# First layer of a four-layer graph network: W1 applied before the aggregate, row statistics tile by tile, attention masks made beside W2

## Chip, cores and metric

One core of a Trainium2 chip. The time is that of one execution on the device, in microseconds. The names of five engines recur: TensorE (PE; its weight loads are PEld), VectorE (DVE), ScalarE (ACT), GpSimd (POOL) and SyncE (SP), which here issues every DMA.

## The reference, cut to what matters

1250 nodes with 512 features, 40000 edges. Four layers follow each other; each takes h = relu(layernorm(x)) and adds its result to x. Only the first and the masks of the second matter here:

```python
h = jnp.maximum(_layernorm(x, axis=-1), 0.0)
agg = jax.ops.segment_sum(h[dst], src, num_segments=n)   # layer 0
y = (1.0 + eps) * h + agg
y = jax.nn.relu(y @ W1.T + b1)
y = y @ W2.T + b2
x = x + layernorm(y) * gamma + beta
# layer 1: softmax over the edges of a node, with q, k, v from relu(layernorm(x))
e = jnp.einsum('ehd,ehd->eh', k[src], q[dst]) / np.sqrt(DK)
```

The sum over edges is linear: with C the 1250x1250 matrix of edge counts, y = ((1 + eps) I + C) h, and so y W1 = ((1 + eps) I + C) (h W1).

## The kernel before, in words

The nodes lie in T = 10 tiles of 128 rows (the last has 98). Everything is f32 but the one-hot rows of the build. Each engine has its own program, executed in its order; they meet at semaphores. All DMAs go through SyncE's one queue in the order of its program.

**Setup (0 to 57 us).** SyncE loads the edges, constants, all of x and W1 (L287 to L309). VectorE (L869 to L985) works out from the edge list which edges each of 80 windows of the count matrix needs: casts, compares, ranges, 32 one-hot rows (L912), three products with parts of the edge weights over 125x10240 (L942). Small matmuls (L421 to L446) help it. ScalarE makes Exp of the weights and copies the keys (L1241, L1244), then for all tiles the row sums of x (L1250), behind VectorE's mean for all tiles (L947) all squares (L1254), one root (L1257), and, behind VectorE's reciprocal (L966), all ten Relu rows into H (L1261).

**Build (57 to 284 us).** For 40 groups of four half-windows TensorE multiplies one-hot rows (L459), VectorE makes the rows just ahead (L1000, L1008), ScalarE copies windows out of PSUM into buffers in X (L1285), SyncE moves each to DRAM (`edge_parts`, L317) and reads the counts back into CD (L326, L328).

**Aggregate (284 to 370 us).** TensorE multiplies H by the counts with 1 + eps on the diagonal (L493), for each of the four feature blocks f in three banks of PSUM; ScalarE copies each into `at` (L1292). Beside it GpSimd adds, tile by tile, the three parts of the edge weight sums (L1454, L1456); SyncE loads them (L332) and writes them back (`edge_sums`, L353). The stage buffers alternate, three in X and three in R0.

**W1 (371 to 405 us).** `feature_major` (L497, L504) multiplies `at` by W1, ScalarE evicts with Relu and bias into HT (L1306). In the gaps ScalarE computes Ln of the counts (L1300, into one of four buffers `lnc_raw`) and VectorE turns them into the additive masks of layer 1 (L1040, L1041), in place in CD. VectorE first puts the diagonal back (L1036).

**W2 with its tail (406 to 485 us).** `node_tiles` (L510 on) loops over the tiles: W2 matmuls of tile t (L531) into four banks in turn, the transposes of h of tile t-6 (L569), the V projection of tile t-7 (`values`, L587). VectorE's loop (from L1065) does per iteration t: add b2 out of PSUM (L1070) and statistics of tile t, the scale of t-1, gamma of t-2 (L1061), statistics of x of t-3, its scale of t-4. ScalarE's `tail` (L1327 on): root of t (L1267), Identity with scale of t-1 (L1314), root of x of t-3, Relu of x of t-4 (L1274), copy of the transposes of t-6 (L1322), copy of V of t-7 (L1349). GpSimd adds beta and updates x (L1462, L1465). x had been overwritten by window buffers and stage buffers, and is loaded again (`x_back`).

At 485.5 us the Q and K projections of layer 1 begin (L597); layers 1 to 3 aren't touched by the change.

Of the kernel before, what the change touches and what calls it, by code (L numbers as in the profile page):

```python
# [74 lines left out]
def rows(t):  # L75
    return min(P, N - t * P)
# [21 lines left out]
def build(nc, A, out):  # L98
# [4 lines left out]
    with ExitStack() as ctx:  # L103
# [52 lines left out]
        def bank(b, n=BANK):  # L156
# [14 lines left out]
        stage = [[X[:, :, :].rearrange("p t o -> p (t o)")[:, q * NQ:(q + 1) * NQ] for q in range(3)],  # L171
                 [R0[:, o:o + NQ] for o in (2048, 8840, 10092)]]
# [89 lines left out]

        def m_at(t):

            return (4 * BANK + t * 256) if t < 4 else (t - 4) * 256
# [17 lines left out]
        def _(sp):  # L283
            def rep(name, n):
                return A[name].rearrange("(a n) -> a n", a=1).to_broadcast([P, n])

            sp.dma_start(srcI, A["src_cols"]).then_inc(sem("edges_in"), 16)  # L287
            sp.dma_start(dstI, A["dst_cols"]).then_inc(sem("edges_in"), 16)
            sp.dma_start(ew, A["weight_cols"]).then_inc(sem("edges_in"), 16)
            sp.dma_start(growI, A["dst_rows"]).then_inc(sem("edges_in"), 16)  # L290
            sp.dma_start(K1[:, :], A["k1"][:, 0:NK1]).then_inc(sem("edges_in"), 16)
            sp.dma_start(K2, A["k2"]).then_inc(sem("edges_in"), 16)
            sp.dma_start(iota, A["iota"]).then_inc(sem("edges_in"), 16)
            sp.dma_start(key_base, A["k1"][:, NK1:NK1 + 2 * NW]).then_inc(sem("edges_in"), 16)
            def load_x(name):
                sp.dma_start(X[:, 0:T - 1, :], A["x"][0:(T - 1) * P, :].rearrange("(t p) f -> p t f", p=P))\
                    .then_inc(sem(name), 16)
                sp.dma_start(X[0:rows(T - 1), T - 1, :], A["x"][(T - 1) * P:N, :]).then_inc(sem(name), 16)

            load_x("x_in")  # L300
            sp.dma_start(bias_col[:, 0:4], A["L0_b1"]).then_inc(sem("x_in"), 16)
            sp.dma_start(bias_col[:, 4:6], A["L1_b1"]).then_inc(sem("x_in"), 16)
            sp.dma_start(bias_col[:, 6:7], A["L0_eps"].to_broadcast([P, 1])).then_inc(sem("x_in"), 16)
            for k in range(2):
                sp.dma_start(bias_col[:, 7 + k:8 + k], A["L2_bm"][k * P:(k + 1) * P].rearrange("(p o) -> p o", o=1))\
                    .then_inc(sem("x_in"), 16)


            sp.dma_start(wa4, A["L0_W1T"].rearrange("(k p) o -> p k o", p=P)).then_inc(sem("l0_w1_in"), 16)  # L309
# [31 lines left out]
            sp.wait_ge(sem("l0_h"), T)  # L341
            load_parts(0)


            sp.wait_ge(sem("base_used"), BASES * NG)
            sp.dma_start(wb4, A["L0_W2T"].rearrange("(k p) o -> p k o", p=P)).then_inc(sem("l0_w2_in"), 16)
            for i, n in enumerate(("L0_b2", "L0_gamma", "L0_beta")):
                sp.dma_start(bc0[:, i, :], rep(n, D)).then_inc(sem("l0_bc_in"), 16)

            load_parts(1)  # L350
            for t in range(T):
                sp.wait_ge(sem("tile_summed"), t + 1)
                sp.dma_start(dram_w[t * P:(t + 1) * P, :], stage[t % 2][0][:, 0:N]).then_inc(sem("w_out"), 16)  # L353
                if t + 2 < T:
                    sp.wait_ge(sem("w_out"), 16 * (t + 1))
                    load_parts(t + 2)
                elif t == T - 2:
                    sp.wait_ge(sem("w_out"), 16 * (t + 1))
                    sp.wait_ge(sem("eps_out"), T)
                    load_x("x_back")  # L360


            sp.wait_ge(sem("l0_h1_ps"), KF)
# [9 lines left out]
            load_qk(1)  # L373
            sp.wait_ge(sem("l0_mm"), T)
# [9 lines left out]
            for i, n in enumerate(("L1_ln1_g", "L1_ln1_b", "L1_ln2_g", "L1_ln2_b", "L1_b2")):  # L384
                sp.dma_start(bc1[:, i, :], rep(n, D)).then_inc(sem("l1_bc_in"), 16)
# [1153 lines left out]
```

## Time and profile before

| | us |
|---|---|
| median of 3 runs (1258.36 to 1259.93) | 1258.97 |
| profiled execution | 1256.01 |
| its span, first to last instruction | 1254.1 |
| TensorE busy | 1102.4 (88%) |
| VectorE busy | 646.8 (52%) |
| ScalarE busy | 419.7 (33%) |
| GpSimd busy | 144.0 (11%) |
| mean granted clock of TensorE | 0.954 of 2.4 GHz |

A busy share over the whole span says little, since the stages have different limits; the rows further down are read stage by stage. The chain of waits follows, from the last instruction back, what released each step. Idle time of an engine off that chain costs nothing.

### The profile page before, as it was taken

The page shows a single profiled execution, that of the slowest core. Times are in us where ns is not written, and L with a number is a line of the kernel's source. Part 1 is how long each engine was busy: PE and PEld are TensorE (multiplying, and loading weights), DVE is VectorE, ACT ScalarE, POOL GpSimd, SP SyncE. Part 2 cuts the span into 40 slices and gives each one's busy share as a digit, 9 for nine tenths or more (in the row PEclk, how much of TensorE's full clock was granted, in tenths as well). Part 3 has the DMA queues.
Part 4 walks back from the last instruction along what each step waited for, and adds up shares of the span by engine and source line. Part 5 has one row for each costly group of instructions (what it writes and reads, how often), then busy time and mean ns, then how long its engine had stood idle before and what let it go on. Part 6 is the DMA issues. An engine that isn't in the chain of part 4 may idle for free.

```text
span 1254.1 us, 17427 instructions
## 1 busy us (share of the span) xinstructions
PE 1102.4 (88%) x5880; PEld 698.9 (56%) x5880; DVE 646.8 (52%) x1835; ACT 419.7 (33%) x711; POOL 144.0 (11%) x112
## 2 busy tenths in 40 slices
PE   1378877779999999989999999999996998899998
PEld 0134444445555445547777777776453798555543
DVE  6877787784017840026666666665619525700033
ACT  2501233330006341016555555555234523610000
POOL 0000000002654440000000000001315403000000
PEclk9998777779999999999999999999999998999999
DMA  5001467778886111100000000005301005000001
GB/s 153 0 0 42 129 173 208 201 213 269 274 281 210 56 34 34 34 0 1 2 1 2 1 1 2 2 1 178 119 1 34 9 13 194 34 1 1 9 33 40
DMA packets 67233, 93.65 MB, mean 75 GB/s; under 512 B 5145, under 2 KB 56032, under 8 KB 67158
## 3 DMA queue, kind: packets, MB, share of 16 engines
q1 hardware_dynamic: 67158, 92.65, 23.4%
q8 instruction: 48, 0.79, 0.3%
q14 instruction: 27, 0.22, 0.1%
HBM read 58.03 MB, written 34.60 MB: 74 GB/s over the span
## 4 chain that ended last, share of the span: by engine, by line
PE 72%; DVE 12%; DMA 6%; issue 5%; ACT 3%; SPq 2%; DVEq 0%; ACTq 0%
PE PS L459 8%; PE PS L669 7%; PE PS L493 7%; PE PS L652 7%; PE PS L817 7%; PE PS L626 7%; PE PS L852 5%; DMA edge_parts<-X 5%; PE PS L597 5%; PE PS L531 5%; PE PS L504 3%; PE PS L587 3%; DVE R L1117 2%; PE PS L779 2%; PE PS L799 2%
## 5 line engine op out<-in xcount | busy, mean ns | idle before, releaser
L459 PE MATMUL PS<-HT,R 125*128 125x313 bf16 (+1 forms) x636 | 178.5, 419 | 61.2 <-DVE HT L1000 27.5
L459 PEld LDWEIGHTS PS<-HT,R 125*128 x636 | 103.5, 171 | 137.0 <-issue 103.9
L1106 DVE CUSTOM_DVE_ANT_0 HT<-PS,CD 128x1250 f32<-128x1250 f32 (+1 forms) x80 | 116.3, 1454 | 55.2 <-issue 55.2
L652 PE MATMUL PS<-K,HT 128*128 128x128 f32 (+2 forms) x800 | 112.5, 280 | 15.0 <-DVE R L1117 14.4
L1008 DVE TENSOR_SCALAR HT<-BC,HT 125x314 f16 x316 | 102.0, 364 | 35.9 <-PE PS L459 30.9
L1382 ACT ACTIVATE HT<-HT,soft 128x1250 f32<-128x1250 f32 (+1 forms) x80 | 107.1, 1338 | 19.7 <-DVE soft L1109 12.6
L1285 ACT COPY X<-PS 128x626 f32<-128x626 f32 x80 | 53.6, 689 | 167.9 <-PE PS L459 102.9
L652 PEld LDWEIGHTS PS<-K,HT 128*128 128x128 f32 (+2 forms) x800 | 84.0, 140 | 43.1 <-DVE R L1117 23.6
L1362 ACT COPY R<-PS 128x512 f32<-128x512 f32 (+1 forms) x120 | 64.8, 574 | 121.5 <-PE PS L652 119.5
L626 PE MATMUL PS<-R 64*128 64x512 f32 (+3 forms) x480 | 95.8, 531 | 4.8 <-DVE soft L1106 3.1
L669 PE MATMUL PS<-R 128*64 128x128 f32 (+2 forms) x1600 | 94.3, 273 | 0.0
L493 PE MATMUL PS<-CD,H 128*128 128x512 f32 (+2 forms) x240 | 86.0, 521 | 3.7 <-issue 3.7
L669 PEld LDWEIGHTS PS<-R 128*64 128x64 f32 (+1 forms) x1600 | 84.8, 137 | 6.4 <-issue 5.8
L1117 DVE COPY R<-PS 128x512 f32<-128x512 f32 (+1 forms) x80 | 54.3, 678 | 65.2 <-PE PS L652 65.2
L817 PE MATMUL PS<-R,H 128*128 128x512 f32 (+2 forms) x240 | 85.2, 513 | 0.0
L1000 DVE TENSOR_SCALAR HT<-BC 125x314 bf16<-125x314 f16 x320 | 72.8, 299 | 13.9 <-PE PS L459 9.7
L626 PEld LDWEIGHTS PS<-R 64*128 64x128 f32 (+1 forms) x480 | 61.2, 185 | 32.0 <-issue 23.3
L1228 DVE SCALAR_TENSOR_TENSOR R<-PS,invdeg,BC 128x512 f32<-128x512 f32 (+1 forms) x10 | 7.5, 749 | 132.9 <-PE PS L852 132.9
L493 PEld LDWEIGHTS PS<-CD,H 128*128 128x128 f32 (+1 forms) x240 | 46.1, 192 | 43.4 <-issue 43.2
L597 PE MATMUL PS<-HT,R 128*128 128x512 f32 (+1 forms) x192 | 67.3, 513 | 0.0
L817 PEld LDWEIGHTS PS<-R,H 128*128 128x128 f32 (+1 forms) x240 | 45.0, 190 | 38.7 <-issue 38.4
L597 PEld LDWEIGHTS PS<-HT,R 128*128 128x128 f32 x192 | 36.5, 190 | 31.2 <-issue 31.1
(211 smaller groups left out, 1357.1 us busy)
## 6 DMA issues: line engine op xcount, KB each, us to landing
edge_parts<-X SPq DMA_DIRECT2D x160, 156.5 KB, 3.5
X<-edge_parts SPq DMA_DIRECT2D x15, 626.0 KB, 5.6
R<-edge_parts SPq DMA_DIRECT2D x15, 626.0 KB, 5.7
CD<-edge_sums SPq DMA_DIRECT2D x1, 6250.0 KB, 20.9
CD<-edge_parts SPq DMA_DIRECT2D x10, 469.5 KB, 4.5
CD<-edge_parts SPq DMA_DIRECT2D x3, 1565.0 KB, 11.6
X<-in_x SPq DMA_DIRECT2D x2, 2304.0 KB
edge_sums<-X SPq DMA_DIRECT2D x5, 625.0 KB, 6.2
```

Of the source, the lines that this page charges most:

```text
L459: return mm(bank(b0 + h, QUART), stat, hot, start=first, stop=True, skip_group_check=True)
L493: i = mm(bank(b0 + j, sn), H[0:rows(t), t, f * P:(f + 1) * P], cd[0:rows(t), t, s0:s0 + sn], start=t == 0, stop=t == T - 1, skip_group_che ...
L597: i = mm(bank(3 * m + j, sn), wqk[p % 2][:, m, k, :], ht[:, k, s0:s0 + sn], start=k == 0, stop=k == KF - 1)
L626: i = mm(PS[0:n, a * N + s0:a * N + s0 + sn], qT[a * DK:(a + 1) * DK, p, t * P:t * P + n], kT[a * DK:(a + 1) * DK, p, s0:s0 + sn], start=T ...
L652: m = nc.tensor.transpose(PS[0:rows(j), o:o + n], Pb[u % 2][a][0:n, j * P:j * P + rows(j)], ident[0:n, 0:n])
L669: m = mm(PS[a * DK:(a + 1) * DK, o:o + n], V[0:rows(j), j, (2 * p + a) * DK:(2 * p + a + 1) * DK], PT[c % RING][0:rows(j), (2 * jj + a) * ...
L817: i = mm(bank(3 * (f % 2) + j, sn), H[0:rows(t), t, f * P:(f + 1) * P], cs[0:rows(t), t, s0:s0 + sn], start=t == 0, stop=t == T - 1)
L1000: ve.tensor_scalar(src_oh[:, base_slot(w, q * GH + h), :], iota[0:EC, :], base_key[:, q, v:v + 1], None, ALU.is_equal).then_inc(sem("base_ ...
L1008: i = ve.tensor_scalar(late_oh[:, bass.ds(m & (GEN - 1), 1), h, :].rearrange("p a n -> p (a n)"), iota[0:EC, :], key_base[0:EC, v:v + 1], ...
L1106: ve.tensor_tensor_reduce(Pb[s][a][0:n], PS[0:n, a * N:(a + 1) * N], cd[0:n, t, :], 1.0, -3e38, ALU.add, ALU.max, soft[0:n, s, a:a + 1]).t ...
L1117: ve.tensor_copy(PT[c % RING].rearrange("p (j n) -> p j n", j=4)[:, :, 0:n], bank(6 + c % 2).rearrange("p (j n) -> p j n", j=4)[:, :, 0:n])\
L1382: sc.activation(Pb[s][a][0:n], Pb[s][a][0:n], ACT.Exp, bias=soft[0:n, s, 2 + a:3 + a], accum_out=zsum[0:n, z + a:z + a + 1]).then_inc(sem( ...
```

## The change

- The setup's loads are reordered: edges and x in parts (tiles 0 and 1, then W1, then tiles 2 to 4, then the rest); iota and key bases come last.
- Row statistics tile by tile: ScalarE sum, square and root, GpSimd the mean and its product with the reciprocal, VectorE the reciprocal (`unit_scale`), ten calls spread through its setup. The products L942 are cut in halves, a `unit_scale` between each pair.
- W1 moves: each tile of h is transposed (`turn_h`), copied to `h_t` and multiplied by W1, ten tiles, with the setup's small matmuls between them; ScalarE copies the result over H. `feature_major` is gone. The aggregate's eviction is the Relu with bias, straight into HT.
- ScalarE's Exp and key copies come after the fifth iteration of its loop over tiles.
- The build begins with banks 4 to 7; its second group waits for all ten tiles of h W1.
- The Ln calls stand in `tail` of W2 (`beside=lnc`), one per tile, and VectorE's mask of tile t at the end of its iteration t.
- The stage buffers of the sums lie in R0 alone, so tiles 0 to 6 of x are loaded again right behind the last counts; the weights of V, Q and K are loaded before the loop of the sums.

The diff, cut to its core:

```diff
+            def turn_h(t):
+                n = rows(t)
+                pe.wait_ge(sem("l0_h"), t + 1)
+                if t > 0:
+                    pe.wait_ge(sem("h_t"), t)
+                for k in range(KF):
+                    i = nc.tensor.transpose(bank(3)[:, k * P:k * P + n], H[0:n, t, k * P:(k + 1) * P], ident[0:n, 0:n])
+                i.then_inc(sem("h_t_ps"), 1)
+
+            pe.wait_ge(sem("l0_w_in"), 16)
+            turn_h(0)
+            for t in range(T):
+                n = rows(t)
+                if t + 1 < T:
+                    turn_h(t + 1)
+                pe.wait_ge(sem("h_t"), t + 1)
+                if t >= 2:
+                    pe.wait_ge(sem("hw"), t - 1)
+                for k in range(KF):
+                    i = mm(bank(t % 2)[0:n], h_t[t % 2][:, k, 0:n], wa4[:, k, :], start=k == 0, stop=k == KF - 1)
+                i.then_inc(sem("hw_ps"), 1)
+                if t == 1:
+                    ranges()
+                if t == 2:
+                    trips_per_group()
+                if t == 3:
+                    trip_ends()
+                if t == 5:
+                    gathered_keys()
...
+                if w == 1:
+                    pe.wait_ge(sem("hw"), T)
...
+            def unit_scale(t):
+
+                n = rows(t)
+                dve.wait_ge(sem("x_std"), t + 1)
+                ve.reciprocal(x_std[0:n, t:t + 1], x_std[0:n, t:t + 1]).then_inc(sem("x_rstd"), 1)
...
+                for h in range(2):
+                    j = 2 * SUB * h
+                    i = ve.tensor_tensor(dst_oh[0:EC, (q + 1) * 4 * SUB + j:(q + 1) * 4 * SUB + j + 2 * SUB, :],
+                                         dst_oh[0:EC, j:j + 2 * SUB, :], wpart[q].unsqueeze(1).to_broadcast(shape), ALU.mult)
+                    if h == 0:
+                        unit_scale(7 + q)
...
+            def mask(t):
+
                 n = rows(t)
                 dve.wait_ge(sem("lnc_raw"), t + 1)
...
+                if t < T:
+                    mask(t)
+            dve.wait_ge(sem("lnc"), T)
...
+            for t in range(T + 5):
+                if t < T:
+                    n = rows(t)
+                    act.wait_ge(sem(x_part(t)[0]), x_part(t)[1])
+                    sc.activation(H[0:n, t, :], X[0:n, t, :], ACT.Copy, accum_out=x_sum[0:n, t:t + 1]).then_inc(sem("x_sum"), 1)
+                if 1 <= t <= T:
+                    u = t - 1
+                    n = rows(u)
+                    act.wait_ge(sem("x_nmean"), u + 1)
+                    sc.activation(H[0:n, u, :], X[0:n, u, :], ACT.Square, bias=x_nmean[0:n, u:u + 1],
+                                  accum_out=x_sq[0:n, u:u + 1]).then_inc(sem("x_sq"), 1)
+                    act.wait_ge(sem("x_sq"), u + 1)
+                    sc.activation(x_std[0:n, u:u + 1], x_sq[0:n, u:u + 1], ACT.Sqrt, scale=1.0 / D, bias=gate[0:n, 1:2])\
+                        .then_inc(sem("x_std"), 1)
+                if 2 <= t < T + 2:
+                    u = t - 2
+                    n = rows(u)
+                    act.wait_ge(sem("x_norm"), u + 1)
+                    sc.activation(H[0:n, u, :], X[0:n, u, :], ACT.Relu, bias=x_nmr[0:n, u:u + 1], scale=x_std[0:n, u:u + 1])\
+                        .then_inc(sem("l0_h"), 1)
+                if 3 <= t < T + 3:
+                    u = t - 3
+                    n = rows(u)
+                    act.wait_ge(sem("h_t_ps"), u + 1)
+                    if u >= 2:
+                        act.wait_ge(sem("hw_ps"), u - 1)
+                    sc.copy(h_t[u % 2][:, :, 0:n], bank(3).rearrange("p (k n) -> p k n", k=KF)[:, :, 0:n])\
+                        .then_inc(sem("h_t"), 1)
+                if 4 <= t < T + 4:
+                    u = t - 4
+                    n = rows(u)
+                    act.wait_ge(sem("hw_ps"), u + 1)
+                    sc.copy(H[0:n, u, :], bank(u % 2)[0:n]).then_inc(sem("hw"), 1)
+                if t == 4:
+                    weights()
...
-                sc.copy(at[:, f, 0:N], PS[:, 3 * (f % 2) * BANK:3 * (f % 2) * BANK + N]).then_inc(sem("l0_agg_ev"), 1)
+                sc.activation(ht[:, f, 0:N], PS[:, 3 * (f % 2) * BANK:3 * (f % 2) * BANK + N], ACT.Relu,
+                              bias=bias_col[:, f:f + 1]).then_inc(sem("l0_h1_ev"), 1)
...
-            tail("l0", "l1_xn", "l1_h", lag=LAG0, after=v_out)
+            tail("l0", "l1_xn", "l1_h", beside=lnc, lag=LAG0, after=v_out)
...
+            def center(t):
+                n = rows(t)
+                pool.wait_ge(sem("x_rstd"), t + 1)
+                gp.tensor_tensor(x_nmr[0:n, t:t + 1], x_nmean[0:n, t:t + 1], x_std[0:n, t:t + 1], ALU.mult)\
+                    .then_inc(sem("x_norm"), 1)
+
+
+
+            for t in range(T):
+                n = rows(t)
+                pool.wait_ge(sem("x_sum"), t + 1)
+                gp.tensor_scalar(x_nmean[0:n, t:t + 1], x_sum[0:n, t:t + 1], -1.0 / D, None, ALU.mult)\
+                    .then_inc(sem("x_nmean"), 1)
+                if t >= 1:
+                    center(t - 1)
+            center(T - 1)
```

## Rows read from the trace of the kernel before

**Rows 1.** Stretches: span, busy PE, PEld, DVE, ACT, POOL, clock, DMA share, GB/s

```profile
290.00:300.00 10.00, 10.00 (x29) 5.23 (x28) 5.78 (x35) 0.00 (x0) 0.41 (x1) 1.00 1.02 354
...
406.40:485.50 79.10, 75.42 (x201) 34.72 (x202) 43.70 (x125) 32.06 (x61) 25.74 (x20) 0.98 0.12 40
...
438.00:441.00 3.00, 3.00 (x5) 1.19 (x4) 1.90 (x7) 1.99 (x5) 2.20 (x2) 0.53 0.02 5
```

**Rows 2.** Chain that ended last, in order of time: start, us, what

```profile
369.81 1.21 ACT R L1292
371.15 33.83 PE PS L504 x96
...
406.45 13.98 PE PS L531 x32
...
446.31 0.44 PE PS L569 x4
446.75 3.44 PE PS L587 x8
...
485.50 67.16 PE PS L597 x192
```

**Rows 3.** Timeline of the setup: start, us, engine, line, operation [idle before]

```profile
16.48 0.49 DVE L890 SCALAR_TENSOR_TENSOR HT<-HT 125x320 f32<-125x320 f32 x1
...
20.50 0.63 ACT L1250 ACTIVATE H<-X 128x512 f32<-128x512 f32 x1
...
41.98 0.72 ACT L1254 ACTIVATE H<-X,invdeg 128x512 f32<-128x512 f32 x1 [15.25 <-DVE invdeg L947]
...
57.21 1.29 PE L459 MATMUL PS<-HT,R 125*128 125x313 bf16 x4 [16.83 <-DVE HT L1000]
```

**Rows 4.** Groups by shape, 406 to 485.5 us: busy us, mean ns

```profile
L531 PE MATMUL PS<-R,HT 128*128 128x512 f32 x72 | 31.5, 593 | 1.5 <-ACT HT L1306 1.5
...
L1349 ACT COPY R<-PS 128x512 f32<-128x512 f32 x9 | 5.3, 586 | 13.1 <-PE PS L587 13.1
```

**Rows 5.** Group by shape, 0 to 57 us: busy us, mean ns

```profile
L446 PE MATMUL PS<-CD 128*125 128x320 f32 x4 | 2.5, 780 | 1.5 <-DVE CD L936 1.5
```

**Rows 6.** TensorE's timeline in the build and in the W2 stage

```profile
103.48 4.26 PE L459 MATMUL PS<-HT,R 125*128 x16 [0.38 <-issue]
...
437.51 5.37 PE L587 MATMUL PS<-WA,HT 128*128 128x512 f32 x8 [2.48 <-ACT HT L1322]
```

**Rows 7.** Who waited for whom, 160 to 284 us: total, times, longest

```profile
ACT X L1285 <- DMA edge_parts<-X: 64.8, 44, 4.0
```

**Rows 8.** ScalarE's timeline around the two table loads

```profile
381.22 1.28 ACT L1300 ACT_TABLE_LOAD   x1
382.52 3.80 ACT L1300 ACTIVATE R<-CD,gate 128x1250 f32<-128x1250 f32 x3
...
407.55 1.28 ACT L1267 ACT_TABLE_LOAD   x1
```

**Rows 9.** GpSimd's timeline: the last tile's sums

```profile
387.37 3.75 POOL L1454 TENSOR_TENSOR R<-R 128x1252 f32<-128x1252 f32 x1 [4.98 <-DMA R<-edge_parts]
391.20 3.30 POOL L1456 TENSOR_TENSOR R<-R 128x1252 f32<-128x1252 f32 x1
```

**Rows 10.** Timeline of the W2 stage: an add and its Identity

```profile
413.59 0.69 DVE L1070 TENSOR_TENSOR R<-PS,BC 128x512 f32<-128x512 f32 x1 [0.40 <-PE PS L531]
...
415.72 0.81 ACT L1314 ACTIVATE R<-R,rs 128x512 f32<-128x512 f32 x1
```

**Rows 11.** VectorE's timeline: the masks

```profile
383.89 0.81 DVE L1040 TENSOR_SCALAR CD<-CD 128x1250 f32<-128x1250 f32 x1 [9.81 <-ACT R L1300]
384.73 1.46 DVE L1041 TENSOR_TENSOR CD<-CD,R 128x1250 f32<-128x1250 f32 x1
...
388.33 3.47 DVE L1040 TENSOR_SCALAR CD<-CD 128x1250 f32<-128x1250 f32 x1
391.83 3.99 DVE L1041 TENSOR_TENSOR CD<-CD,R 128x1250 f32<-128x1250 f32 x1
```

More of the change, by code:

```diff
@@ new lines, in gathered_keys @@
+            def gathered_keys():
+                pe.wait_ge(sem("setup_dve"), 9)
+                for k in range(3):
+                    i = mm(bank(4)[0:EC, 0:FIX * 2 * NW], key_t[0:KC[k], k, :], pick[0:KC[k], k, :, :], start=k == 0, stop=k == 2)
+                i.then_inc(sem("setup_ps"), 1)
+            def turn_h(t):
[6 more added lines that the diff above has]
+                i.then_inc(sem("h_t_ps"), 1)
@@ L929, in _ @@
             link(ve.tensor_copy(wpart[2], rem2))
+            unit_scale(6)
             dve.wait_ge(sem("setup_ps"), 6)
@@ L1237, in _ @@
             sc = nc.scalar
-            act.wait_ge(sem("setup_dve"), 5)
-            sc.activation(we, ew, ACT.Exp, bias=wmx[:, 3:4]).then_inc(sem("we"), 1)
-            act.wait_ge(sem("setup_ps"), 4)
-            for k in range(3):
-                i = sc.copy(key_t[0:KC[k], k, :], bank(3)[0:KC[k], k * P:k * P + EC])
-            i.then_inc(sem("key_t"), 1)
-            act.wait_ge(sem("x_stats_free"), 1)
-            act.wait_ge(sem("x_in"), 7 * 16)
-            for t in range(T):
-                n = rows(t)
-                sc.activation(H[0:n, t, :], X[0:n, t, :], ACT.Copy, accum_out=x_sum[0:n, t:t + 1]).then_inc(sem("x_sum"), 1)
@@ L1251, in _, with weights @@
-            act.wait_ge(sem("x_nmean"), 1)
-            for t in range(T):
-                n = rows(t)
-                sc.activation(H[0:n, t, :], X[0:n, t, :], ACT.Square, bias=x_nmean[0:n, t:t + 1],
-                              accum_out=x_sq[0:n, t:t + 1]).then_inc(sem("x_sq"), 1)
-            act.wait_ge(sem("x_var"), 1)
-            sc.activation(x_std[:, :], x_sq[:, :], ACT.Sqrt).then_inc(sem("x_std"), 1)
-            act.wait_ge(sem("x_norm"), 1)
-            for t in range(T):
-                n = rows(t)
-                sc.activation(H[0:n, t, :], X[0:n, t, :], ACT.Relu, bias=x_nmr[0:n, t:t + 1], scale=x_std[0:n, t:t + 1])\
-                    .then_inc(sem("l0_h"), 1)
+            def weights():
+                act.wait_ge(sem("setup_dve"), 5)
+                sc.activation(we, ew, ACT.Exp, bias=wmx[:, 3:4]).then_inc(sem("we"), 1)
+                act.wait_ge(sem("setup_ps"), 4)
+                for k in range(3):
+                    i = sc.copy(key_t[0:KC[k], k, :], bank(5)[0:KC[k], k * P:k * P + EC])
+                i.then_inc(sem("key_t"), 1)
```

185 lines of the change are left out of this document (83 added, 102 removed).

## The prediction

> **What bounds the kernel now.** I read the table by stage first [rows 1]: in every stage from 57 us to the end TensorE is the busiest engine, but the chain of waits [rows 2] shows which stretches are really TensorE's. From 371.15 on it is, for 33.83 us: the matmuls of W1 (L504) run without a gap, then comes an eviction, and the W2 stage starts at 406.45. That stage ends when the projection starts, at 485.50, so it lasts 79.05 us; it is TensorE's by volume (75.4 us busy [rows 1]). Before 57 us the chain is VectorE's: the build's first matmul, at 57.21, had waited 16.83 us for it [rows 3]. So three stretches count: the setup (0 to 57.2), the W1 stage (371.3 to 406.45) and the W2 stage with its tail (79.05). The profiled execution took 1256.01 us (span 1254.1); the median of the timed runs is 1258.97, 2.96 more, and I add each change to both.
>
> **1. W1 leaves the path.** Today the aggregate's last eviction ends at 371.0, W1 starts at 371.15, W2 at 406.45 [rows 2]. After the change the aggregate's last eviction is already the Relu with bias (some 0.1 us longer) and W2 can start at 371.3. Gone: 35.2 us. The aggregate itself keeps its 240 instructions and its banks: 0.
>
> **2. The setup gets W1.** Ten tiles, each four transposes and four matmuls of 128x512 in two passes. Dense, a tile's eight matmul instructions take 3.44 us and four transposes 0.44 [rows 2]. At this place TensorE is slow, though: a two-pass matmul of 320 columns took 780 ns [rows 5], where 512 columns took 593 in the W2 stage [rows 4]; so the clock is at 1.2 GHz here, although the table prints 1.00 for it. The restart at 437.51 shows what dense work does then: eight instructions in 5.37 us [rows 6] at a granted clock of 0.53 [rows 1], the eight at 446.75 in 3.44 again [rows 2]. I take the first tile at 6.8, later ones at 3.44.
> TensorE executes in order, and all ten tiles stand ahead of the first group of the build, which starts at 57.21 today. ScalarE does per tile a sum (0.63), a square (0.72), a short root, the Relu (0.81, as the Identity of [rows 10]) and two copies out of PSUM (0.59 each) [rows 3, 4], about 3.6 us with the wait for its own accumulator; with three loads of the function table (1.28 each [rows 8]) for root, Exp and root, that is 40 us of its own. The first Relu waits for VectorE's first reciprocal (its place is ahead of the operation at 16.48 [rows 3]) and ends near 18; transposes, copy and a load of the third tile of x bring the first W1 matmul to 21.6. From there TensorE's queue holds 10 x 3.44 + 9 x 0.44 = 38.4 us, the small setup matmuls that are now between the tiles (eight for the ranges, four for the trips, two for the ends and six for the keys, some 6.4 by the 0.78 of [rows 5] for the six largest and their overlap), 2.4 of waits and 3.4 for the slow first tile: 72.2; of this the gathered keys give back about 1 at full clock. **The build starts near 71 instead of 57.2, +14**. VectorE doesn't cover this: its own chain ends 5 us later than now, because its fifth reciprocal waits for a root that ScalarE does behind the Exp and the key copies, and each of the ten reciprocals stands in front of work of the build's setup. The few small steps that VectorE loses and the two inputs fewer that it waits for save about 1, which is in the 5. Bounds: +9.5 (all tiles at full clock, no waits) to +22 (three tiles slow, waits twice as long). GpSimd's new 128x1 operations have no row; between nothing and 3.30 us, its row of 1252 columns [rows 9], and I take 0.2. The chain meets it twice, for the first and the last tile, so the start moves by 0 to 6; the upper bound holds that.
>
> **3. The build passes this on.** From 160 us on ScalarE waits for the window transfers, 64.8 us in 44 waits [rows 7], but a transfer can't begin before its window is built, so the late start isn't taken up there. The steps of the build are short groups of four matmuls with register work between; what a warmer TensorE gives them I count at 0 (at most 1 or 2 us, in the lower bound). The +14 arrives at the aggregate. Waiting for `hw` ahead of the second group costs nothing, since sixteen matmuls of the first group still run at 103.48 [rows 6].
>
> **4. The masks move into the W2 tail.** This is the largest term. Today Ln and masks lie beside W1: ScalarE loads the Ln table once at 381.22 and the root's at 407.55 [rows 8]. So Ln and root are in different tables, and a switch costs its load (381.22 to 382.50, Ln at 382.52). In the tail each tile has root, Identity, Ln, root: two loads per tile, twenty in all. Now the order of VectorE and ScalarE in one iteration, timed from VectorE's add on the PSUM bank (L1070): statistics, root and scale, then Identity from +2.13 to +2.94 (413.59, 415.72) [rows 10], load +1.28, Ln +1.27 (3.80 for three) [rows 8] gives +5.5; only then VectorE's mask, 0.81 and 1.46 [rows 11]; then the next add. With 0.1 of signalling **the iteration takes 7.85 us, where W2's matmuls need 3.44** [rows 2]. The second load and VectorE's remaining steps fit beside it. Of the two loads one is exposed.
> The sum: first add 3.7 after W2's start; ten iterations, the first without Identity, 77.5; then the values still to be done. TensorE's order is W2 tile t, transposes t-6, values t-7, and the values wait for a copy that ScalarE makes behind Ln; so values 3 to 9 lie behind the tenth iteration: 0.5 + 7 x 3.88 - 0.44 = 27.2. Together 108.4.
> To that comes GpSimd. The fourth iteration waits for its first update of x. Its sums end at 394.5 now; ahead of their loads now stand seven tiles of x (1.8 MB) and the V, Q and K weights (2 MB), while the queue already moves 354 GB/s [rows 1], some 11 us of transfer, of which I count 7.5 (the loop of sums waits on round trips and absorbs part), and 2 for GpSimd's operations that are stretched beside VectorE's, to 3.75 for one [rows 9]. At 404 it is free, the update is there at 406.7, the mask behind it 4.5 later than otherwise: +4.5 (0 to 10).
> VectorE and GpSimd hold each other up: the mask operations of 0.81 and 1.46 took 3.47 and 3.99 while the sums ran [rows 9, 11], +5.2 for one pair. Three pairs meet the sums, most of which ends in the wait just counted; later GpSimd's pair for the tile ends about when the mask begins. I take +3 (0 to 10).
> TensorE idles 22 us ahead of its eighth tile, 8 ahead of the first values and 4 ahead of the fourth; a restart costs 5.37 - 3.44 = 1.9 [rows 2, 6]. Two on the path, +3.8 (0 to 6), though one of today's is in the 79.05.
> **Tail: 108.4 + 4.5 + 3 + 3.8 = 119.7, against 79.05: +40.6** (+29 to +55).
>
> The Trainium skill, "SBUF — State Buffer" (SBUF: two separate sides), says that VectorE and GpSimd share one pair of ports and that an operation of the one that needs it holds it whole while the other blocks; by that the 3.47 and 3.99 are waits, not slower work, and the trace agrees: the first ends just behind the end of GpSimd's operation.
> The Trainium skill's "ScalarE: Activation LUTs" (What ACT_TABLE_LOAD costs; table sets) advises to do all calls of one set before switching, and prices a switch at about 2.66 us, 1.28 of load and 1.38 of drain. The rule speaks against this change; its load agrees with 1.28 here, its drain doesn't show between 381.22 and 382.52. By its price the tail would be an estimated 14 us longer.
>
> **Sum.** +14 - 35.2 + 40.6 = +19.4: 1275.4 for a profiled execution, **1278 us** for the median.
>
> **Rivals.**
> (a) *The masks fit into idle time.* For it: in the W2 stage VectorE is busy 43.7 of 79.1 us and ScalarE 32.1 [rows 1]; the moved work is 23 us on one and 13 + 23 on the other. If the engines ran ahead enough, the tail would grow by only some 6: 14 - 35.2 + 6 = -15, 1244 us. Against: each add stands behind the mask of the tile before in VectorE's order. 11 in 100.
> (b) *One of the costs is hidden:* the loads don't appear or lie in waits (ten exposed at 1.28: -12.8), or the setup's delay is taken up in the build (-14). 1265 us. 10 in 100.
> (c) *TensorE stays at 1.2 GHz through the setup.* Ten tiles at 6.9 + 0.8 put the start of the build at about 103: +46 instead of +14, 1310 us. It decides if the third tile still takes over 6 us. For it: sixteen matmuls in a row of 313 columns took 0.266 each at 103.48 [rows 6], which is 1.2 GHz, after 46 us of building without a pause of note. Against: those were short groups with gaps; dense matmuls woke up in one tile. 7 in 100.
> (d) *Both loads are exposed,* because the second root of the iteration is what the next add waits on: 10 x 1.28 more, 1291 us. 8 in 100.
> My forecast, 1262 to 1296 by its bounds, has 64 in 100.
>
> **Numbers.** Range 1260 to 1296: it leaves out (a) and (c), 18 in 100, and the sum of all upper bounds. About 0.2% (2.5 us) can be told from no change. Faster: (a) and a little of (b), 0.12. Same: the rest of (b) at its lower bounds, 0.04. Slower: 0.84.
>
> **What would show it.** The build's first matmul at 67 to 75 us; no L504, W2 starting 1.5 us behind the aggregate; twenty table loads in the tail and the adds at L1070 about 7.9 us apart for ten tiles; the projection starting some 115 to 122 us behind W2's start. Adds 4 to 5 us apart would mean (a), and my reading of the order was wrong; fewer loads (b); a third W1 tile over 6 us (c). If the aggregate starts less late than the build does, step 3 is wrong.

## The result: 27 us slower

The changed kernel takes 1285.32 us (median of four runs, 1284.29 to 1286.84) against 1258.66 us (1256.12 to 1259.93) for the kernel before on the same chip: ratio 1.0214, 95% interval 1.0193 to 1.0235. The forecast was 1278 us with a range of 1260 to 1296, so sign and range hold and the predicted time is 7.3 us too low. The profiled execution took 1285.58 us (span 1283.8) against 1256.01: +29.6, of which 2.7 is that the profiled run of before lay under its median.

**The profile after.** The table by stretch has the same columns as [rows 1]; the first stretch is what the setup grew by, the second a piece of it, the third the W2 stage with its tail.

```profile
57.21:76.72 19.51, 14.83 (x35) 6.62 (x34) 8.56 (x19) 4.63 (x8) 4.38 (x2) 0.83 0.00 0
...
64.00:69.00 5.00, 5.00 (x7) 1.98 (x7) 3.25 (x12) 0.58 (x1) 0.00 (x0) 0.57 0.00 0
...
390.70:515.04 124.34, 83.85 (x201) 37.70 (x202) 75.47 (x147) 67.69 (x89) 48.53 (x28) 0.82 0.25 82
```

In [rows 1] the W2 stage had TensorE busy for 75.4 of 79.1 us. Now it is busy for 84 of 124, VectorE for 75 and ScalarE for 68: no engine fills the stage, so it is an order of waits that sets it. The chain of waits shows which (start, us, what; it answers to [rows 2]).

```profile
398.00 1.28 ACT L1369
399.30 1.35 ACT R L1369
400.67 1.91 DVE CD L1084
402.60 3.98 DVE CD L1085
...
418.57 2.51 DVE rs L1022
...
439.38 1.28 ACT L1369
440.67 1.35 ACT R L1369
442.04 0.82 DVE CD L1084
442.88 1.46 DVE CD L1085
...
460.51 5.54 PE PS L620 x8
...
485.70 6.61 PE PS L620 x8
...
515.04 1.29 PE PS L630 x3
```

L1369 is the load of the Ln table and Ln itself, L1084 and L1085 are the masks, L1022 is a product of one column in VectorE's scale, L620 the V projection, L630 the projection that ends the stage. The chain that was TensorE's runs through ScalarE and VectorE for ten tiles. Where the 29.5 us up to the projection come from:

| stretch | before | after | difference | predicted |
|---|---|---|---|---|
| first matmul of the build | 57.21 | 76.72 | +19.5 | +14 |
| build, to the aggregate's start | 226.6 | 225.9 | -0.7 | 0 |
| aggregate and W1, to W2's start | 122.66 | 88.11 | -34.55 | -35.2 |
| W2 stage, to the projection | 79.05 | 124.34 | +45.3 | +40.6 |
| projection to the end of the span | 768.6 | 768.8 | +0.2 | 0 |

Two terms were too small, the setup by 5.5 us and the tail by 4.7. Both shortfalls have to do with GpSimd. For the setup, the timeline of the changed kernel (start, us, engine, line, operation, idle before):

```profile
50.26 2.80 DVE L992 TENSOR_TENSOR R<-R,BC 125x5120 bf16<-125x5120 bf16 x1
...
53.07 5.53 DVE L992 TENSOR_TENSOR R<-R,BC 125x5120 bf16<-125x5120 bf16 x2
53.22 8.36 POOL L1512 TENSOR_TENSOR valid<-invdeg,winv 128x1 f32<-128x1 f32 x2 [3.16 <-DVE winv L910]
...
58.60 2.79 DVE L992 TENSOR_TENSOR R<-R,BC 125x5120 bf16<-125x5120 bf16 x1
...
61.48 0.81 ACT L1314 ACTIVATE H<-X,valid,winv 128x512 f32<-128x512 f32 x1 [7.42 <-POOL valid L1512]
...
62.91 1.09 PE L473 MATMUL PS<-K,H 128*128 128x128 f32 x4 [4.68 <-ACT CD L1322]
...
63.79 5.86 PE L486 MATMUL PS<-WA,CD 128*128 128x512 f32 x8
...
69.83 7.06 PE L486 MATMUL PS<-WA,CD 128*128 128x512 f32 x16
...
76.72 1.53 PE L509 MATMUL PS<-HT,R 125*128 125x313 bf16 x10
```

GpSimd's product of one column (`center`, L1512) starts behind the ninth reciprocal and two of them take 8.36 us, until VectorE's last wide product has ended. The line's own view has the shortest, median and longest of its ten in ns:

```profile
L1512 POOL TENSOR_TENSOR valid<-invdeg,winv x10: 184/190/8224, 16.5 to 61.4; 128x1 f32<-128x1 f32 x9, 98x1 f32<-98x1 f32 x1
```

So the first of the two alone took 8.22 us and the second began at 61.4. ScalarE's Relu, which needs only the first, waits 7.42 us for it, TensorE waits 4.68, restarts near its lower level (granted clock 0.57 from 64 to 69 us, eight matmuls in 5.86 instead of 3.60 us), and still has two tiles ahead of the build.

### The profile page after: what moved, and what is told of

Same layout as the page of the kernel before. It is cut to its first block, busy times and chain, and to the rows that moved or that the text cites. A ratio compares the mean times of both kernels' runs of the same rounds, so it can differ in the third digit from the quotient of the medians.

```text
span 1283.8 us, 17580 instructions
## 1 busy us (share of the span) xinstructions
PE 1117.5 (87%) x5904; PEld 703.7 (55%) x5904; DVE 654.8 (51%) x1845; ACT 453.7 (35%) x756; POOL 160.4 (12%) x132
## 4 chain that ended last, share of the span: by engine, by line
PE 69%; DVE 12%; ACT 6%; DMA 6%; issue 5%; SPq 1%; POOL 1%; DVEq 0%; ACTq 0%
PE PS L509 8%; PE PS L702 7%; PE PS L542 7%; PE PS L685 7%; PE PS L850 7%; PE PS L659 6%; PE PS L885 5%; PE PS L630 5%; DMA edge_parts<-X 5%; PE PS L564 3%; PE PS L620 3%; DVE R L1163 2%; PE PS L812 2%; PE PS L832 2%; PE PS L486 2%
## 5 line engine op out<-in xcount | busy, mean ns | idle before, releaser
L509 PE MATMUL PS<-HT,R 125*128 125x313 bf16 (+1 forms) x636 | 176.1, 415 | 46.0 <-ACT X L1353 15.5
L1042 DVE TENSOR_SCALAR HT<-BC 125x314 bf16<-125x314 f16 x320 | 73.0, 299 | 16.0 <-PE PS L509 12.3
L630 PE MATMUL PS<-HT,R 128*128 128x512 f32 (+1 forms) x192 | 67.3, 513 | 0.0
L1529 POOL TENSOR_TENSOR R<-R 128x1252 f32<-128x1252 f32 x10 | 28.3, 2832 | 304.6 <-DMA R<-edge_parts 304.6
```

The lines of the kernel that those rows point to most:

```text
L509: return mm(bank(b0 + h, QUART), stat, hot, start=first, stop=True, skip_group_check=True)
L630: i = mm(bank(3 * m + j, sn), wqk[p % 2][:, m, k, :], ht[:, k, s0:s0 + sn], start=k == 0, stop=k == KF - 1)
L1042: ve.tensor_scalar(src_oh[:, base_slot(w, q * GH + h), :], iota[0:EC, :], base_key[:, q, v:v + 1], None, ALU.is_equal).then_inc(sem("base_ ...
```

## The experiments

All kernels below state the bound of the register on which the build waits by an assertion (`nc.s_assert_within(...)` instead of `.with_bounds(...)`). The first run, the changed kernel with nothing else, prices that and is what the others are compared with. The kernel before, timed beside them on each chip, took between 1258.4 and 1262.1 us (medians), so runs on different chips are compared by their ratios to it. "Stage" is the time from W2's first matmul to the projection's first in the timeline of the profiled execution; the timeline lets the projection start 0.16 us earlier than the chain, so the changed kernel's stage is 124.2 by this measure.

**control**

```diff
-                     v[VALUES * k + GH].with_bounds(min_val=w + k + 2, max_val=(w + k + 1) * (NC - FIX) + 1))
+                     nc.s_assert_within(v[VALUES * k + GH], min_val=w + k + 2, max_val=(w + k + 1) * (NC - FIX) + 1))
```

> The changed kernel itself, with one more assertion behind each load of a group's end in the build (40 groups, on TensorE and VectorE), which all kernels of these experiments carry. Every theory: within 0.2% of the changed kernel, 1283 to 1288 us, iterations of the W2 stage 7.83 us apart, the build's first matmul at 76.7. If it is faster or slower, the other experiments are read against it.

1288.8 us, ratio 1.0256 (1.0222 to 1.0289), 0.4% above the changed kernel's 1.0214 where at most 0.2% was expected. The build starts at 76.7 us as without the assertion, the aggregate 5.8 us later, and the stage is 121.3 us, 2.9 shorter: its first add comes 1.5 earlier and the intervals beside the sums are 0.9 shorter. So much a stage that collides with the sums varies from one kernel to the next.

**before_with_assertion**: the same edit in the kernel before.

> The kernel before with the bound of the register read in the build stated by an assertion, as in all these experiments, and nothing else: it prices what masks_in_tail_only carries. The control took 3.5 us over the changed kernel for it. If the assertion costs the build the same here, 1261 to 1264 us; in masks_in_tail_only the aggregate began 7.2 us later than in the kernel before, which would rather give 1264 to 1267 us.

1266.76 us beside 1262.05, ratio 1.0039 (1.0028 to 1.005). W2 starts at 415.3 and the stage is 78.9 us. So assertion against assertion the change costs 1.0256 / 1.0039 = 1.022, what it costs without (1.0214).

**masks_in_tail_only**: the kernel before with `mask(t)` at the end of the tail's loop on VectorE and `beside=lnc` in ScalarE's tail, W1 where it was.

```diff
-            for t in range(T):
+            def mask(t):
...
-            dve.wait_ge(sem("lnc"), T)
...
+                if t < T:
+                    mask(t)
...
-            tail("l0", "l1_xn", "l1_h", lag=LAG0, after=v_out)
+            tail("l0", "l1_xn", "l1_h", beside=lnc, lag=LAG0, after=v_out)
```

> The kernel before, with one part of the change alone: Ln in ScalarE's tail and the mask at the end of VectorE's iteration. Theory A (order: each add waits for the mask of the tile before, and that for root, Identity, table load and Ln): iterations 7.8 us apart for ten tiles, W2 stage 108 + 2 to 4 of restarts = 110 to 112 us instead of 79, so +31 to +33, 1290 us; here the sums of GpSimd end ahead of W2, so they can't be the cause. Rival B (the stage grew because GpSimd's sums and VectorE block each other): hardly any sum is left in the stage, it stays under 90 us, at most 1270 us. Rival C (the masks fit into idle time): 85 us, 1265 us.

1297.86 us, ratio 1.0317 (1.0284 to 1.035). W2 starts at 415.0, as in before_with_assertion, and the stage grows from 78.9 to 111.7 us. VectorE's timeline, masks and adds (L1070) of this kernel:

```profile
441.41 0.68 DVE L1070 TENSOR_TENSOR R<-PS,BC 128x512 f32<-128x512 f32 x1
...
447.02 0.81 DVE L1041 TENSOR_SCALAR CD<-CD 128x1250 f32<-128x1250 f32 x1 [1.92 <-ACT R L1303]
447.87 1.46 DVE L1042 TENSOR_TENSOR CD<-CD,R 128x1250 f32<-128x1250 f32 x1
449.24 0.69 DVE L1070 TENSOR_TENSOR R<-PS,BC 128x512 f32<-128x512 f32 x1
```

The adds are 7.83 us apart with W1 in its old place and the sums over 14 us before the stage begins; 111.7 is 3.3 more than the 108.4 that the prediction had for the bare order, ahead of its 3.8 for TensorE's restarts. The order of root, Identity, load, Ln and mask makes the pace, by itself. Masks in idle time (rival a, some 6 us) and both loads exposed (rival d, some 9.1 us an iteration) fall.

**ln_as_identity**

```diff
-                sc.activation(lnc_raw[t % 4][0:n], cd[0:n, t, :], ACT.Ln, bias=gate[0:n, 0:1]).then_inc(sem("lnc_raw"), 1)
+                sc.activation(lnc_raw[t % 4][0:n], cd[0:n, t, :], ACT.Identity, bias=gate[0:n, 0:1]).then_inc(sem("lnc_raw"), 1)
```

> The changed kernel with Identity in place of Ln (layer 1's masks leave the logarithm of the counts out; the operation's length is the same), so no function table changes in the W2 stage. Theory A with one exposed load per iteration: adds 6.55 us apart instead of 7.83, -12.8 us, 1272 us. Rival D (both loads of an iteration are exposed): 5.3 us apart, -25.6 us, 1260 us. Rival E (loads lie in waits): 7.8 apart, 1285 us.

1280.84 us, ratio 1.019 (1.0161 to 1.022), 8.0 us under the control; the expected 12.8 don't come. The adds stand 7.46 apart instead of 7.84, though a load of 1.28 is out of each iteration. Control first, then ln_as_identity (groups by shape on VectorE beside W2's tiles; busy us, mean ns):

```profile
L1084 DVE TENSOR_SCALAR CD<-CD 128x1250 f32<-128x1250 f32 x6 | 5.7, 952 | 11.1 <-ACT R L1369 11.1
```

```profile
L1084 DVE TENSOR_SCALAR CD<-CD 128x1250 f32<-128x1250 f32 x6 | 11.2, 1858 | 2.6 <-ACT R L1369 2.0
```

And the timeline of ln_as_identity, GpSimd's update of x and the mask:

```profile
434.96 1.26 POOL L1542 TENSOR_TENSOR X<-X,R 128x512 f32<-128x512 f32 x1
435.04 1.86 DVE L1084 TENSOR_SCALAR CD<-CD 128x1250 f32<-128x1250 f32 x1 [0.50 <-ACT R L1369]
```

The mask now begins 0.08 us after GpSimd's update of x began, and takes 1.86 us instead of 0.81: it ends 0.68 behind GpSimd's end. In the control the load held the mask back until GpSimd was done (its update ran from 436.56 to 437.82, the mask began at 438.07). The mask begins 1.43 us earlier in its iteration and takes 1.05 longer, so the iteration is 0.38 shorter. One load per iteration is on the path, as predicted, but it covered a collision. Most of what the run gained lies elsewhere. The stage is 8.5 us shorter, of which 1.4 lie in the eighth interval and 3.8 behind the tenth add. There TensorE waits 1.38 us ahead of the fourth value tile and 1.54 ahead of the fifth, instead of 3.70 ahead of the fourth, and the fourth takes 3.70 us instead of 6.43.

**sums_of_4_columns**: GpSimd's sums of the count parts run over 4 columns instead of 1252.

```diff
-                gp.tensor_tensor(s[0], s[0], s[1], ALU.add).then_inc(sem("sum_own"), 1)
+                gp.tensor_tensor(s[0][:, 0:4], s[0][:, 0:4], s[1][:, 0:4], ALU.add).then_inc(sem("sum_own"), 1)
```

> The changed kernel, with GpSimd's additions of the edge weight parts done on 4 of 1252 columns (the weights of layer 2 are left incomplete); loads and write-backs stay. Theory A plus port: the first three iterations shrink from 10.56, 10.15 and 11.95 us to 7, 7.9 and 7.9, the ten copies that restore the diagonal from 6.7 to 3 to 4 us: -9 to -13 us, 1274 us. Rival (those three are long for another reason, as the first update of x coming late behind its loads): under -4 us.

1282.61 us, ratio 1.0207 (1.0177 to 1.0237), 6.2 us under the control, between the two expectations; the stage is 113.7 us, 7.6 shorter. The 9 to 13 were worked out from the changed kernel, and the control loses 2.3 us less than it to collisions (its first add and the three intervals). The first three intervals are 6.97, 7.83 and 7.84 us, but the fourth is 9.41: there GpSimd's first two operations on x meet VectorE's one-column product (1.13 instead of 0.16 us) and its mask (1.42 instead of 0.81). Its first mask pair on VectorE, and behind it the same pair in the changed kernel:

```profile
402.22 0.81 DVE L1084 TENSOR_SCALAR CD<-CD 128x1250 f32<-128x1250 f32 x1 [2.92 <-ACT R L1369]
403.06 1.46 DVE L1085 TENSOR_TENSOR CD<-CD,R 128x1250 f32<-128x1250 f32 x1
```

```profile
400.67 1.90 DVE L1084 TENSOR_SCALAR CD<-CD 128x1250 f32<-128x1250 f32 x1 [2.92 <-ACT R L1369]
402.60 3.98 DVE L1085 TENSOR_TENSOR CD<-CD,R 128x1250 f32<-128x1250 f32 x1
```

**loads_earlier_alone**: SP's queue loads parts 1 and 2 of a sum as soon as their buffers are free, and x and the projection weights inside the loop of sums instead of ahead of it.

```diff
-            load_x(0, 7, "x_in0")
...
                 if t + 2 < T:
+                    load_parts(t + 2, (1, 2))
                     sp.wait_ge(sem("w_out"), 16 * (t + 1))
-                    load_parts(t + 2)
+                    load_parts(t + 2, (0,))
+                if t == 3:
+                    load_x(0, 7, "x_in0")
...
```

> The changed kernel with only the queue reordered as in and_loads_earlier; the masks stay in the W2 tail, nothing is left out. GpSimd's last sum should end some 12 us after W2's start (11.8 in all_three) instead of 31. Theory A (the masks set the tail's pace from the fourth tile on, the collisions with the sums only lengthen the first three iterations): iterations two and three lose the 2.3 to 3.7 us that each has over 7.84, the later ones stay 7.84 apart, the stage falls from 121.3 to 113 to 117 us and the run to 1280 to 1285 us, so the reordering is worth 16 us with the masks gone and only a third of that with them. Theory B (the tail waits for the sums' end even with the masks in it): the gain is the same 14 to 18 us, 1271 to 1275 us.

1285.45 us, ratio 1.0184 (1.0161 to 1.0207) against the control's 1.0256. The last sum ends 12.3 us behind W2's start (403.8) instead of 31.3, and the adds are 9.81, then 7.82 and 7.84 apart: the stage is 114.8 us, 6.5 shorter. In the profiled executions the projection starts at 518.6 us, in the control at 518.2, because the build is longer here, and the profiled execution (1290.18) is the slowest of its four (1282.75 to 1290.18); so the 0.7% that the run gains by its ratio can't be laid to the stage. GpSimd's timeline, its last sum and the first operation of the tail:

```profile
412.86 3.28 POOL L1534 TENSOR_TENSOR R<-R 128x1252 f32<-128x1252 f32 x1
428.06 1.26 POOL L1540 TENSOR_TENSOR R<-R,BC 128x512 f32<-128x512 f32 x1 [11.93 <-DVE R L1108]
```

GpSimd now waits 11.93 us for VectorE. With the masks in the tail, early sums are worth only the collisions that they avoid.

**masks_beside_projection**: Ln and masks move behind the tail, beside the Q and K projections, with two buffers for the logarithms.

```diff
-                if t < T:
-                    mask(t)
+            for t in range(2):
+                mask(t)
             for p in range(PAIRS):
                 dve.wait_ge(sem("k_ps"), p + 1)
                 ve.tensor_copy(kT[:, p, 0:N], PS[:, 3 * BANK:3 * BANK + N]).then_inc(sem("k_ev"), 1)
+                for t in ((2, 3, 4), (5, 6, 7), (8, 9), ())[p]:
+                    mask(t)
...
```

> The changed kernel with the masks taken out of the W2 tail and made beside the Q and K projections, where ScalarE and VectorE have only the evictions; nothing is left out of the computation. Theory A (the tail's pace is set by the masks): the adds after the third come some 4 to 6 us apart instead of 7.84, and the stage's end is then set by the sums of x, which end 33 us after W2's start and need nine more value tiles after them: about 97 us instead of 121.3 in the control, so the run falls by 24 us less what the masks give back beside the projections (0 to 8): 1265 to 1273 us. Theory B (the tail is set by the late loads of x and of the sums, not by the masks): the stage stays within 5 us of the control's and the run near 1285 us or above it.

1265.39 us, ratio 1.0037 (1.002 to 1.0053), 2.1% (27.5 us) under the control. The stage falls from 121.3 to 95.2 us. The first four adds are 3.36 to 3.44 apart, then one gap of 21.65 us comes, until x is updated, then three of 3.95 to 3.97. The sums' late end was hidden behind the masks and is the bound once they are gone. The table by stretch, the projections alone (columns as above):

```profile
495.50:562.40 66.90, 66.90 (x192) 36.28 (x191) 26.29 (x23) 19.32 (x16) 0.00 (x0) 1.00 0.10 32
```

TensorE is busy without a gap while VectorE works 26.3 and ScalarE 19.3 us beside it. The projections take 67.2 us with the masks beside them and without. From their start to the end of the span it is 770.2 us against the control's 769.1, so in this place the masks cost 1.1 us at most.

**and_loads_earlier**: masks_beside_projection with the queue of loads_earlier_alone.

> masks_beside_projection, and the queue reordered: the parts of the third and later sums are loaded as soon as their buffers are free, and x and the projection weights are loaded within the sums instead of ahead of them. If the sums' late end is what holds the tail once the masks are gone, the stage falls from about 97 to the 79 to 85 us that it had before the change, and the run by 10 to 18 us more: 1250 to 1262 us. If the sums are held by GpSimd's own time (two passes of about 3 us for each of ten tiles) and not by the loads, the run stays within 4 us of masks_beside_projection.

1249.7 us, ratio 0.9912 (0.9894 to 0.993); the stage is 79.6 us, about as long as before the change (78.9). The same reordering that took 6.5 us off the stage with the masks in it takes 15.6 us off without them.

**center_on_dve**: the product of one column follows VectorE's reciprocal on VectorE.

```diff
-                ve.reciprocal(x_std[0:n, t:t + 1], x_std[0:n, t:t + 1]).then_inc(sem("x_rstd"), 1)
+                link(ve.reciprocal(x_std[0:n, t:t + 1], x_std[0:n, t:t + 1]))
+                ve.tensor_tensor(x_nmr[0:n, t:t + 1], x_nmean[0:n, t:t + 1], x_std[0:n, t:t + 1], ALU.mult)\
+                    .then_inc(sem("x_norm"), 1)
```

> The changed kernel with the 128x1 product of the x statistics done by VectorE right behind its reciprocal instead of by GpSimd; nothing is left out. If GpSimd's small product, kept from the SBUF port by VectorE's products (8.36 us for two), is what makes the build start late, the first build matmul comes at 70 to 73 us instead of 76.7 and the run is 4 to 7 us under the control: 1282 to 1285 us. If the setup is late because of TensorE's lower clock or the later transfers, it stays within 1.5 us of the control's 1288.8 us.

1285.74 us, ratio 1.0203 (1.0186 to 1.022), 0.5% (6.7 us) under the control by the ratios. The timeline of the setup:

```profile
54.82 0.14 DVE L910 RECIPROCAL winv<-winv 128x1 f32<-128x1 f32 x1
55.00 0.16 DVE L911 TENSOR_TENSOR valid<-invdeg,winv 128x1 f32<-128x1 f32 x1
...
63.71 7.06 PE L486 MATMUL PS<-WA,CD 128*128 128x512 f32 x16
70.60 1.46 PE L509 MATMUL PS<-HT,R 125*128 125x313 bf16 x9
```

The product takes 0.16 us here and the build starts at 70.60, 6.1 us earlier. From 41 us on TensorE's tiles now follow each other almost without a gap.

**quarter_of_w1_product**: center_on_dve with one of the four feature blocks of the W1 product.

```diff
-                for k in range(KF):
-                    i = mm(bank(t % 2)[0:n], h_t[t % 2][:, k, 0:n], wa4[:, k, :], start=k == 0, stop=k == KF - 1)
+                i = mm(bank(t % 2)[0:n], h_t[t % 2][:, 0, 0:n], wa4[:, 0, :], start=True, stop=True)
```

> center_on_dve with three of the four feature blocks of the W1 product left out in the setup (2 matmuls for each tile instead of 8; the values are then wrong in that sense, the rest of the work is the same). Per tile TensorE loses 2.6 us, 26 us for the ten. If TensorE's stream sets the setup's end once the small product is off GpSimd, the build starts as soon as VectorE is ready, whose last setup operations end 64.3 us in center_on_dve and whose first build operation could start 2.5 to 3 us later: 67 to 68.5 us instead of 70.6, and the run is 2 to 3.5 us under center_on_dve's 1285.7. If TensorE sets nothing there, the start stays at 70.6 us; if TensorE also delays what VectorE waits for (its small products queue behind the tiles), the start falls below 66 us and the run below 1281 us.

1278.27 us, ratio 1.0129 (1.0106 to 1.0152), 0.7% (9.3 us) under center_on_dve. By its numbers it is the third outcome of the three: the build starts at 62.5 us, 8.1 earlier, so TensorE's tiles also delay what VectorE waits for. VectorE's and TensorE's timelines:

```profile
62.01 0.94 DVE L1043 TENSOR_SCALAR HT<-BC 125x314 bf16<-125x314 f16 x4 [2.53 <-issue]
...
62.47 1.01 PE L508 MATMUL PS<-HT,R 125*128 125x313 bf16 x4 [1.38 <-DVE HT L1043]
```

It is not TensorE's small products that VectorE waits for, as the expectation had it, but ScalarE's roots. Its reciprocals (`unit_scale`) in center_on_dve, ScalarE's copy of h W1 ahead of the second of these roots, and the first of the two reciprocals with a quarter of W1, where the second doesn't wait:

```profile
34.08 0.16 DVE L910 RECIPROCAL winv<-winv 128x1 f32<-128x1 f32 x1 [4.33 <-ACT winv L1310]
...
43.50 0.16 DVE L910 RECIPROCAL winv<-winv 128x1 f32<-128x1 f32 x1 [1.93 <-ACT winv L1310]
```

```profile
41.16 0.59 ACT L1330 COPY H<-PS 128x512 f32<-128x512 f32 x1 [2.63 <-PE PS L486]
```

```profile
30.74 0.16 DVE L909 RECIPROCAL winv<-winv 128x1 f32<-128x1 f32 x1 [1.25 <-ACT winv L1309]
```

ScalarE copies each tile's product out of PSUM before it goes on to the next sum, square and root, so TensorE's tiles reach VectorE through ScalarE. Here the build waits for VectorE, as in [rows 3], 5.3 us later than in the kernel before. The 19.5 us of the setup are so 6.1 for GpSimd's product, 8.1 for three quarters of the W1 matmuls and 5.3 for what is left (statistics, turns, a quarter of W1, the order of the input loads), which wasn't taken apart.

**all_three**: and_loads_earlier with center_on_dve.

> The three repairs together: masks beside the projections, loads earlier, the small product on VectorE; nothing is left out. If the three costs add up, the run is and_loads_earlier less 4 to 7 us: 1244 to 1256 us, which would be under the kernel before (1258.4 us) although W1 stays in the setup. If one hides behind another, it stays at or above 1258 us.

1240.74 us (1236.48 to 1243.34), ratio 0.9844 (0.9817 to 0.9871): 1.6% faster than the kernel before, with the assertion still in it, and 3 us below the lowest time expected. Its table by stretch, stage and projections:

```profile
389.40:469.40 80.00, 75.28 (x201) 34.61 (x202) 46.05 (x130) 29.64 (x59) 34.44 (x24) 0.98 0.26 82
469.40:536.30 66.90, 66.90 (x192) 36.24 (x191) 26.29 (x23) 19.32 (x16) 0.00 (x0) 1.00 0.10 32
```

That is the stage of [rows 1] again, and the gain of the early W1 stays. The build starts at 68.6 us, 2.0 earlier than in center_on_dve with the same setup. The third W1 tile makes 1.7 of it, center_on_dve first, then all_three:

```profile
35.83 5.29 PE L486 MATMUL PS<-WA,CD 128*128 128x512 f32 x8
```

```profile
35.50 3.60 PE L489 MATMUL PS<-WA,CD 128*128 128x512 f32 x8
```

TensorE had waited 2.7 us ahead of this tile's transposes in both, but the granted clock behind the pause was 0.68 in one, partly the lower level, and 1.00 in the other, the full level. By the clock that this tile gets, GpSimd's product costs the setup 6.1 or 8.15 us; why the clock differs is open.

## Why the prediction held, and where it was short

**What bounds the kernel, and W1's removal** (step 1: -35.2, measured -34.55). The chain's 33.83 us of L504 with the waits around it [rows 2] are gone; the aggregate itself takes 0.6 us longer (86.64 against 86.00 in the chains), where the text had 0.

**The setup** (step 2: +14, measured +19.5). The step that failed is the term for GpSimd's 128x1 operations. It was bounded by nothing and 3.30 us for each and taken at 0.2, with 0 to 6 us on the start; center_on_dve measures 6.1. Without it the build starts at 70.60, and in all_three at 68.57, where the text had "near 71": the work of ten tiles in TensorE's order was sized about rightly. VectorE's chain was not: its first operation of the build starts 7.1 us later than before (63.87 against 56.77), and 10.5 later in center_on_dve, where the text had 5; TensorE's own work hides this in both. That the bound nearly held is luck. It took the price from the widest row of GpSimd, but one operation of one column took 8.22 us. Its duration goes with VectorE's products beside which it stands, and these, the longest operations of the setup, should have been looked up: three of them follow each other there. The Trainium skill, "SBUF — State Buffer" (SBUF: two separate sides), says that the shared port pair is held by whoever is first for its whole operation. The prediction quoted this for the masks and did not apply it to the new product, where by that rule an operation of one column waits like one of a thousand. The product before, which stood beside a single product of VectorE and took 2.69 us, agrees; the one of 8.22 us is longer than one such product (2.8 us), and why it didn't get in between them is not shown.

**The clock** (rival c). The first W1 tile took 6.13 us (predicted 6.8), the second and the third 3.60 in the timeline, so the rival falls. What the text didn't have is the second cold start, 5.86 us, behind the wait for GpSimd.

**The build** (step 3: passes on +14 unchanged; measured 19.5 in, 18.8 out). ScalarE still waits for the window transfers, and the late start is not taken up.

**The tail** (step 4: +40.6, measured +45.3). The iteration was predicted at 7.85 us; the adds are 7.83 to 7.85 apart in five of nine intervals. There are ten loads of the Ln table and ten of the root's; in the chain of waits stand nine of Ln's and two of the root's, ahead of value tiles. The waits in the stage (total, times, longest):

```profile
PE PS L602 <- ACT H L1342: 22.6, 2, 20.3
DVE CD L1084 <- ACT R L1369: 20.7, 10, 3.5
```

The sum was 108.4 + 4.5 + 3 + 3.8. Measured: the first add 5.24 behind W2's start instead of 3.7; the three iterations beside the sums 10.56, 10.15 and 11.95 instead of 6.85 (the first is without Identity) and twice 7.85. With the first add that is 11.65 us over the 108.4, where the text had 7.5 for the late update and the port. The eighth interval is 9.59, and from the tenth add to the projection there are 37.66 instead of 35.05: 4.35 more, where the text had 3.8 for TensorE's restarts. The mis-sized term is the port's. The late update was timed well: the sums end 33.65 us behind W2's start, predicted 32.7, and the first update of x 36.7 behind it, predicted 35.4. But its 4.5 us are not on the path. The collisions had by then moved the fourth add to 37.9, and the statistics of x, 2.6 behind it, find the update there and don't wait. By the durations in this timeline all but 0.2 of the 11.65 are collisions, for which the prediction had 3 us, counted for the mask pairs alone. The copies that restore the diagonal, ahead of the first add, and the one-column operation of VectorE collide too. VectorE's timeline of the changed kernel:

```profile
389.73 6.28 DVE L1078 COPY CD<-X 128x128 f32<-128x128 f32 x7
...
412.11 3.13 DVE L1084 TENSOR_SCALAR CD<-CD 128x1250 f32<-128x1250 f32 x1 [3.53 <-ACT R L1369]
...
418.57 2.50 DVE L1022 SCALAR_TENSOR_TENSOR rs<-mv,rs 128x1 f32<-128x1 f32 x1
...
431.19 0.69 DVE L1014 BATCH_NORM_STATS2 stats<-X 128x6 f32<-128x512 f32 x1
```

In sums_of_4_columns all ten copies take 1.43 us, the first three iterations 6.97, 7.83 and 7.84, and the stage is 7.6 us shorter. The residue of 113.7 is 1.5 from the predicted 108.4 + 3.8, and these 1.5 are the collision of its fourth interval (9.41 instead of 7.85).

**The rivals.** (a) is refuted by masks_in_tail_only. (b) priced ten hidden loads at 12.8; with no load at all only 8 came back, so even its premise would have given less. (d) would need 9.1 us between adds; the one interval over this behind the third, the eighth, waits 1.67 us for TensorE. In sum the terms missed +5.5, -0.7, +0.65 and +4.7, together the 10.1 by which the profiled execution lies over the 1275.4 of the sum; the two large ones are within their bounds and have the same sign, so the range held without one of them covering the other.

**What the change is worth.** Its first part pays: W1 in the setup costs 19.5 us, or 11 to 13 without GpSimd's product, and gives 35. Its second part loses twice the 15.5 that are left, 32.8 us by masks_in_tail_only, and delayed loads and collisions add the rest.

## What to carry to other kernels

Work that fits into an engine's idle share doesn't fit for that: write out the order of each engine for one iteration, and put moved work where the stage is one engine's alone, as beside a projection that keeps TensorE busy and the others idle. When a new small operation goes to GpSimd, ask how long VectorE's operations beside it are, not how long it is itself. A load's or a sum's place in a queue has a price that depends on what hides it: the same reordering gave 6.5 us with the masks in the stage and 15.6 us without.

## What the runs showed of the hardware

- One product of 128x1 on GpSimd took 8.22 us beside three of VectorE's products of 125x5120 (2.8 us each), 2.69 beside one and 0.19 in the median; the same product on VectorE took 0.16. It didn't get in between the first two products, nor at VectorE's reciprocal of 0.14 us ahead of the third.
- VectorE's one-input f32 operation of 128x1250 is hit as well, 0.81 alone and 1.86 us when it began 0.08 us behind a GpSimd operation of 1.26; a one-column operation with two inputs took 2.50 instead of 0.16.
- Taking 1.28 us of table load off the path brought 0.38, since the load had kept the mask out of such a collision.
- With the same setup and behind the same pause of 2.7 us, a tile's eight matmuls took 5.29 us at a granted clock of 0.68 in one kernel and 3.60 at 1.00 in another.
- The build's length, from its first to its last matmul, lay between 225.3 us (sums_of_4_columns) and 235.0 (loads_earlier_alone) among kernels that share its code, with 227.2 in the control. This hides part of the gain of loads_earlier_alone in its run, and its cause was not looked for.
